# A two-layer graph network on one core: x through two DMA queues, fifteen tiles of rows on VectorE, the destination lists on ScalarE, and chunk 0 summed first

## What is computed

```python
h = jnp.maximum(_layernorm(x, axis=-1), 0.0)
deg = segment_sum(ones, src, N);  dinv = where(deg > 0, rsqrt(max(deg, 1)), 0)
norm = -dinv[src] * dinv[dst]
def cheb_conv(x, W0, W1, b):
    tx1 = segment_sum(x[src] * norm[:, None], dst, N)
    return x @ W0 + tx1 @ W1 + b
h = cheb_conv(h, W1_0, W1_1, b1)
h = layer_norm(h, gamma, beta)
h = where(h >= 0, h, 0.01 * h)
return x + cheb_conv(h, W2_0, W2_1, b2)
```

## Time and profile before

| what | value |
|---|---|
| median of 3 runs | 2083.22 us (2079.54 to 2084.0) |
| profiled execution | 2077.38 us, its span 2075.6 us |
| POOL | 1507.3 us busy, 73% of the span |
| PE | 1742.7 us busy, 84% |
| DVE | 776.0 us busy, 37% |
| ACT | 317.4 us busy, 15% |
| DMA | 514.94 MB, 248 GB/s on average |

### The profile page before, as it was taken

How to read it: one execution, slowest core, us unless ns; L and a number is a source line. 1 busy time by engine, 2 the same in 40 slices (tenths; PEclk the granted TensorE clock), 3 DMA queues, 4 the chain that set the end, 5 groups by cost and what they waited for, 6 DMA issues and landing times.

```text
span 2075.6 us, 25930 instructions
## 1 busy us (share of the span) xinstructions
PE 1742.7 (84%) x8740; PEld 666.3 (32%) x8740; DVE 776.0 (37%) x2411; ACT 317.4 (15%) x647; POOL 1507.3 (73%) x1596
## 2 busy tenths in 40 slices
PE   3459888888888888888888988888898888888888
PEld 3433333332323322223333333333333333323333
DVE  9944444444454444444442222212222222222221
ACT  8701111111111111111111111000110101101010
POOL 2277777777777777777777777777777777777775
PEclk9969999999999999999999999999999999999999
DMA  9898888888888888888878888888888888888875
GB/s 262 267 328 250 244 243 242 243 241 241 236 237 241 243 241 238 237 240 241 243 228 260 256 251 256 251 255 249 253 257 248 253 254 253 256 250 256 255 242 182
DMA packets 188714, 514.94 MB, mean 248 GB/s; under 512 B 45271, under 2 KB 46958, under 8 KB 187339
## 3 DMA queue, kind: packets, MB, share of 16 engines
q0 software_dynamic: 128576, 422.78, 69.2%
q1 hardware_dynamic: 56374, 90.16, 12.5%
q10 hardware_dynamic: 3638, 0.42, 0.3%
HBM read 472.40 MB, written 40.84 MB: 247 GB/s over the span
## 4 chain that ended last, share of the span: by engine, by line
POOL 61%; issue 21%; PE 10%; DVE 6%; DMA 1%; ACT 1%; SPq 0%; DVEq 0%; ACTq 0%
POOL arena L560 61%; PE ps L1232 4%; PE ps L1356 4%; DVE w_all L844 2%; DVE work L844 1%; PE ps L1224 1%; DMA scal<-node_scales 0%; DVE ps L1101 0%; ACT arena L689 0%; DMA arena<-table,idx_all 0%; PE ps L1420 0%; DVE stats L1104 0%; DVE ps L1111 0%; DMA node_scales<-scal_all 0%; DVE stats L853 0%
## 5 line engine op out<-in xcount | busy, mean ns | idle before, releaser
L560 POOL DMA_INDIRECT arena<-table,idx_all x1536 | 1454.8, 947 | 470.5 <-issue 467.4
L1356 PE MATMUL ps<-arena,hots 128*32 128x512 f32 x5048 | 729.1, 611 | 135.6 <-DVE hots L1023 77.2
L1356 PEld LDWEIGHTS ps<-arena,hots 128*32 128x32 f32 x5048 | 186.4, 110 | 653.7 <-issue 458.1
L1023 DVE TENSOR_SCALAR hots<-iota_f,loc_all,arena 128x64 f32<-128x64 f32 (+1 forms) x768 | 234.1, 334 | 341.1 <-DMA arena<-table,idx_all 339.9
L1232 PE MATMUL ps<-arena 128*128 128x512 f32 (+1 forms) x432 | 196.6, 597 | 35.8 <-ACT arena L689 35.8
L1232 PE MATMUL ps<-w_all,arena 128*128 128x512 f32 (+1 forms) x432 | 196.1, 597 | 35.8 <-ACT arena L689 35.8
L679 ACT ACTIVATE arena<-ps,scal 128x512 f32<-128x512 f32 x106 | 73.0, 689 | 921.8 <-PE ps L1420 883.6
L1232 PE MATMUL ps<-arena,work 128*128 128x512 f32 (+1 forms) x432 | 199.5, 605 | 0.0
L1232 PE MATMUL ps<-w_all,work 128*128 128x512 f32 (+1 forms) x432 | 193.2, 591 | 0.0
L1140 DVE SCALAR_TENSOR_TENSOR ps<-ps,scal,arena 128x512 f32<-128x512 f32 x52 | 39.5, 759 | 351.1 <-PE ps L1232 351.1
L1224 PE MATMUL ps<-ident,arena 128*128 128x128 f32 x848 | 137.4, 286 | 27.7 <-DMA scal<-node_scales 20.3
(11 more groups left out here) (158 smaller groups left out, 725.9 us busy)
## 6 DMA issues: line engine op xcount, KB each, us to landing
arena<-table SPq DMA_DIRECT2D x106, 256.0 KB, 4.0
arena<-table,idx_all POOLq DMA_INDIRECT x1550, 4.0
table<-arena SPq DMA_DIRECT2D x53, 256.0 KB, 4.0
arena<-in_x_dram SPq DMA_DIRECT2D x53, 256.0 KB, 5.7
out_dram<-arena SPq DMA_DIRECT2D x53, 256.0 KB
table<-arena SPq DMA_DIRECT2D x10, 1124.4 KB
arena<-in_x_dram POOLq DMA_DIRECT2D x9, 1120.0 KB, 34.0
w_all<-in_L_gnn_W_dram SPq DMA_DIRECT2D x2, 1024.0 KB, 14.0
```

Of the source, the lines that this page charges most:

```text
L560: nc.gpsimd.indirect_dma_start(out=rows_of(n, c)[0:rn, 0:RW if L == 0 else D], out_offset=None, in_=table[L][0:NEAR if near else N, :], in ...
L1023: hot = nc.vector.tensor_scalar(hot_of(n, c)[:, cols], iota_f[:, cols], loc, factor_of(i, c), ALU.is_equal, ALU.mult)
L1356: return nc.tensor.matmul(tx_ps[n % 2][strip, :], hot_of(n, c)[:, strip], rows_of(n, c)[:, 0:D], start=start, stop=stop)
```

## The change

It has seven parts.

1. **x by two queues.** POOL loads only the even groups 2 to 10. SP loads group 0 and all the odd ones, in one go at the start, ahead of the first store to the table. The last group of five is split into three and two tiles, so there are 12 groups.
2. **Fifteen tiles on VectorE**, at the steps 1, 2, and 4 to 16; none after step 16. ScalarE keeps 35.
3. **The dst lists** are converted by ScalarE, between the writing of `idx_all` and its first square root.
4. **The tests of the chunks** in `bases()` take 12 instructions in place of 24: half of them treat three chunks of a group at once.
5. **Loads of SP.** The first weight of layer 0 goes out straight after the factors; the own rows of chunks 0 and 1 come next after the flag, then the second weight, then the wait for the stored scales and the loads of scales.
6. **TensorE** sums chunk 0 before it transposes own rows; it waits for the weights only ahead of the first product.
7. **VectorE** makes all 14 one-hots of chunk 0 before `count_first()`.

```diff
-    XG = (0, 2) + tuple(range(5, NT + 1, 5))
+    XG = (0, 2) + tuple(range(5, NT, 5)) + (NT - 2, NT)
     NG = len(XG) - 1
-    DVE_TILES = (4, 9, 14, 19, 24, 29, 34, 39, 44, 49)
+    DVE_TILES = (4, 9, 14, 18, 19, 23, 24, 28, 29, 33, 34, 39, 43, 44, 49)
-    DVE_AT = (2, 4, 7, 9, 11, 14, 16, 18, 21, 23)
+    DVE_AT = (1, 2, 4, 5, 6, 7, 8, 9, 10, 11, 12, 13, 14, 15, 16)
...
+            for g in range(1, NG, 2):
+                for n0, n1 in parts:
+                    sp.dma_start(nodes[n0:n1, XG[g]:XG[g + 1], :], x_rows[n0:n1, XG[g]:XG[g + 1], :],
+                                 max_dma_last_dim=4 * D).then_inc(s_x[g], 16)
...
+            sp.dma_start(weights[0][0], W10.rearrange("(k p) n -> p k n", p=P)).then_inc(s_w[0], 16)
             sp.wait_ge(s_scales, 1)
             sp.dma_start(node_scales.rearrange("(p t) c -> p (t c)", t=NT),
                          scal_all[:, :, :].rearrange("p t c -> p (t c)")).then_inc(s_scal_out, 16)
-            for k, w in enumerate((W10, W11)):
-                if k:
-
-                    sp.wait_ge(s_group, 1)
-                sp.dma_start(weights[0][k], w.rearrange("(k p) n -> p k n", p=P)).then_inc(s_w[0], 16)
...
+            def load_weights():
+                sp.wait_ge(s_group, 1)
+                sp.dma_start(weights[0][1], W11.rearrange("(k p) n -> p k n", p=P)).then_inc(s_w[0], 16)
+                sp.wait_ge(s_scal_out, 16)
...
             sp.wait_ge(s_base, 1)
-            sp.wait_ge(s_scal_out, 16)
             sp.wait_ge(s_tab, 2 * 16 * (NG - 1))
...
                 if L == 0:
-                    load_own(0, 0)
-                    load_own(0, 1)
+                    load_own(0, 0, False)
+                    load_own(0, 1, False)
+                    load_weights()
+                    load_scales(0, 0, first_node(0))
+                    load_scales(1, 1, first_node(1))
...
-            for g in range(1, NG):
+            for g in range(2, NG, 2):
                 for n0, n1 in ((0, TA), (TA, TR)):
                     pool.dma_start(nodes[n0:n1, XG[g]:XG[g + 1], :], x_rows[n0:n1, XG[g]:XG[g + 1], :],
                                    max_dma_last_dim=4 * D).then_inc(s_x[g], 16)
...
-            pool.wait_ge(s_idxps, 1)
-            pool.wait_ge(s_first, 1)
-            pool.wait_ge(s_dsts, 48)
-            nc.gpsimd.tensor_copy(loc_all[:, 0:FB * P], dst_rows[:, 0:FB * P]).then_inc(s_dstrows, 1)
-            nc.gpsimd.tensor_copy(loc_all[0:S - FB * P, FB * P:],
-                                  dst_rows[0:S - FB * P, FB * P:]).then_inc(s_dstrows, 1)
...
+            act.wait_ge(s_first, 1)
+            act.wait_ge(s_dsts, 48)
+            nc.scalar.copy(loc_all[:, 0:FB * P], dst_rows[:, 0:FB * P]).then_inc(s_dstrows, 1)
+            nc.scalar.copy(loc_all[0:S - FB * P, FB * P:], dst_rows[0:S - FB * P, FB * P:]).then_inc(s_dstrows, 1)
             act.wait_ge(s_vdeg, 1)
...
-                    for j in range(4):
-                        at = c + (SHORT + (j - 1) * SLOTS if j else 0)
-                        setup.add(nc.vector.scalar_tensor_tensor(
-                            out=broken[:, :, j], in0=chunk_begin[:, :, j], scalar=float(strip * Q),
-                            in1=slot_edge[:, :, at], op0=ALU.add, op1=ALU.is_gt if after_it else ALU.is_le))
+                    edge = slot_edge[:, :, SHORT:].rearrange("p g (j c) -> p g j c", c=SLOTS)[:, :, :, c]
+                    test = ALU.is_gt if after_it else ALU.is_le
+                    setup.add(nc.vector.scalar_tensor_tensor(
+                        out=broken[:, :, 0], in0=chunk_begin[:, :, 0], scalar=float(strip * Q),
+                        in1=slot_edge[:, :, c], op0=ALU.add, op1=test))
+                    setup.add(nc.vector.scalar_tensor_tensor(
+                        out=broken[:, :, 1:4], in0=chunk_begin[:, :, 1:4], scalar=float(strip * Q),
+                        in1=edge, op0=ALU.add, op1=test))
...
-                        if i == 0 and c == 5:
+                        if i == 0 and c == SHORT - 1:
                             count_first()
...
                     pe.wait_ge(s_fac, 1)
+                    sums(0, 0)
                 transpose_own(L, 0)
                 transpose_own(L, 1)
+                pe.wait_ge(s_w[L], 32)
                 dense_own(L, 0)
                 for i in range(NC):
-                    if i < NC - 1:
+                    if L == 0 and i == 0:
+                        pass
+                    elif i < NC - 1:
                         sums(L, i)
...
-                pe.wait_ge(s_w[0], 32)
                 layer(0)
-                pe.wait_ge(s_w[1], 32)
                 layer(1)
```

More of the change, by code:

```diff
@@ L386, in _, with load_scales, load_own @@
                          scal_all[:, :, :].rearrange("p t c -> p (t c)")).then_inc(s_scal_out, 16)
-            for k, w in enumerate((W10, W11)):
-                if k:
-                    sp.wait_ge(s_group, 1)
-                sp.dma_start(weights[0][k], w.rearrange("(k p) n -> p k n", p=P)).then_inc(s_w[0], 16)
             def first_node(i):
                 return sp.value_load(base_i[0:1, bass.ds(i, 1)], min_val=0, max_val=BASE_MAX)
-            def load_own(L, i):
+            def load_weights():
+                sp.wait_ge(s_group, 1)
+                sp.dma_start(weights[0][1], W11.rearrange("(k p) n -> p k n", p=P)).then_inc(s_w[0], 16)
+                sp.wait_ge(s_scal_out, 16)
+            def load_scales(u, i, first):
+                sp.dma_start(scal[:, bass.ds(i * NSC, NSC)], node_scales[bass.ds(first, P), :]).then_inc(s_own[u], 16)
+            def load_own(L, i, scales=True):
                 u = (L * NC + i) % 2
@@ L399, in load_own @@
                 sp.dma_start(own[u], table[L][bass.ds(first, P), 0:D]).then_inc(s_own[u], 16)
-                if L == 0:
-                    sp.dma_start(scal[:, bass.ds(i * NSC, NSC)],
-                                 node_scales[bass.ds(first, P), :]).then_inc(s_own[u], 16)
+                if L == 0 and scales:
+                    load_scales(u, i, first)
             def load_residual(i):
@@ L590, in _ @@
                               dst[EC:E].rearrange("(p c) -> p c", c=EC)[:, 0:1]).then_inc(s_nxt, 16)
-            dst_rows = dst.rearrange("(p c) -> p c", p=EP)
+            dst_lists = dst.rearrange("(p c) -> p c", p=EP)
             for n0, n1 in ((0, TA), (TA, EP)):
-                act.dma_start(dst_i[n0:n1, :], dst_rows[n0:n1, :]).then_inc(s_dst, 16)
+                act.dma_start(dst_i[n0:n1, :], dst_lists[n0:n1, :]).then_inc(s_dst, 16)
             act.wait_ge(s_const, 1)
```

1 line of the change is left out of this document (added).

## The result

| | before | after |
|---|---|---|
| median of the runs taken together | 2081.99 us (2079.54 to 2084.0, 4 runs) | 2101.88 us (2098.08 to 2104.01, 4 runs) |
| profiled execution, its span | 2077.38 us, 2075.6 us | 2098.08 us, 2096.3 us |
| start of the gathers of chunk 1 | 117.48 us | 138.53 us |

The ratio is 1.0098 [1.0083, 1.0112], with its 95% interval: the change makes the kernel slower by about 1%. The direction was right and the size was not: the loss is 20 us where 6 were forecast, and lies outside the range.

What follows compares the result with a forecast made beforehand. POOL's gathers were taken to set the pace from chunk 1's start at 117.48 us. Terms +5.6 +2.5 -1.0 delay the flag 7.1 us, and 7.1 - 2.3 + 1.3 gives +6.0: 2089.2 us, range 2083 to 2095.

Steps and rivals of the forecast that it cites:

- x through two queues: VectorE ahead of tile 4: it stalls until group 1 lands from SP's queue, +2.5 us on the flag.
- The bound from above: Tile 4's stall: group 1 lands no later than group 2 did before, 16.20 us, so at most 5.6 us.
- I count no second stall: VectorE's tiles after tile 4: later groups of x arrive in time, no further stall.
- Five tiles, +5.6 us: VectorE's histogram: five more tiles at 1.12 us each delay histogram, factors and flag by 5.6 us.
- The histogram end: VectorE's last histogram operation: forecast 8.1 us later than 96.37, at 104.5 us.
- Twelve tests, -1.0 us: VectorE's chunk tests ahead of the flag: 12 instructions in place of 24 save 1.0 us.
- POOL after the flag: POOL's entry into chunk 1: load of the flag and branch come behind a late flag, 1.26 us.
- Level with the flag, hidden behind it by 0.4 us: Factors in the table before chunk 1: landed by 123.1 us, hidden behind POOL's start at 123.5.
- The gathers of chunk 0: POOL's first gather hangs until the histogram ends at 104.5; all end by 121.9, costing and bringing nothing.
- rival C: Table stores behind SP's loads: starved, the table lands after 105 us; +8.6 us, 2092 us, chance 0.14.
- A (no stall): VectorE ahead of tile 4: x is in time; +3.5 us, 2086.7, no change that can be told, chance 0.27.
- B: Layer 0's first chunks: TensorE sets the pace, so summing chunk 0 early gains some 6 us, about 2077; chance 0.11.

Runs made afterwards that it cites:

- run with ten tiles: Changed kernel with VectorE's ten tiles at the steps of before, x still through two queues: 2087.09 us, ratio 1.0039 to the kernel before.
- gathers last: Changed kernel with x by POOL's queue alone and ten VectorE tiles; POOL also waits for the factors before chunk 0's gathers: 2078.28 us, ratio 0.9998 to before.
- the kernel whose gathers wait: Changed kernel where POOL also waits for the histogram's end before chunk 0's gathers: 2098.66 us, ratio 1.0095 to the kernel before.
- one queue: Changed kernel with x loaded by POOL's queue alone, fifteen VectorE tiles kept: 2088.41 us, ratio 1.0051 to the kernel before.
- the order of before: Changed kernel with chunk 0 summed after the own rows' transposes and first product on TensorE: 2098.45 us, ratio 1.0094 to the kernel before.
- the kernel without parts 1 and 2: Changed kernel with x by POOL's queue alone and VectorE's ten tiles at their old steps: 2078.76 us, ratio 1.0002 to the kernel before.
- the kernel with the flag ahead: Changed kernel with x by POOL's queue, nine VectorE tiles, first weight behind the scales, tests ahead of the factors' one-hots: 2076.63 us, ratio 0.999 to before.

## Why the prediction was wrong in size

**The step that failed is "x through two queues", +2.5 us: it measured 14.1.** Three things were wrong in it.

- *The bound from above was none.* It let tile 4 arrive between "as before" and 16.20, the landing of group 2, "since by then the same lists and groups had been moved". But the order of the groups within the queues is what the change alters: by 16.4 us POOL's queue had moved 1.82 MB, group 2 and part of group 4, in place of SP's group 1. The sum that was wanted is by the queue: 1.68 MB stand in SP's queue up to group 1, and the earlier trace rows gave 222 GB/s for all. An estimate with half of that, 111 GB/s, is 15.1 us and an end past 17, a stall of 6.5 us, above the bound of 5.6. Nothing in the rows spoke for the middle of the two.
- *Share and stragglers.* The queue's bytes were through at 16.4 us, a stall of 5.6: its share was less than half (78 GB/s from 5 to 20 us), but it had a start of 0.84 MB by 5 us. The remaining 4.4 us of the 9.98 passed until the last part of the group had landed. The prediction had no term for this lag, though group 2 had one of 2.4 us before.
- *"I count no second stall."* "Each later group 8 us or so" had no row behind it. The first two groups of SP's queue for which VectorE stood, 1 and 3, came 15.6 us apart (20.78 and 36.38), and VectorE asked for group 3 at step 4: 4.12 us.

**Five tiles, +5.6 us: right.** A step with a tile still lasts 4.17 us. The run with ten tiles finds 13.6 us between the ends of the two histograms, 7.9 of them stalls, and leaves 5.6.

**The histogram end** is the sum: 5.6 + 14.1 = 19.7, less 0.5 for the conversion to `counts` behind step 18, which took 0.74 us beside POOL's own conversion and takes 0.21 now that this one is gone; 19.4 measured. The prediction forecast 8.1 and missed the small gain.

**Twelve tests, -1.0 us: right.** They take 1.40 us where the 24 took from 111.26 to 113.52, 2.26: -0.86.

**The flag, from the end of the histogram:** 19.6 us, where 18.8 - 1.0 = 17.8 was forecast: 1.8 us short. In the run with the gathers last it took 18.0, as forecast. In the change 16 matmuls of the spread of the factors (L1282) last 3.75 us where they last 2.10 before. That term was not in the prediction, and its cause stays open (below).

**"POOL after the flag", 1.26 us: it measured 2.15** (the kernel whose gathers wait) and 2.16 (one queue). The nearest row was VectorE's and not POOL's. Before, the flag was there 2.3 us ahead of chunk 1, so by this step it was ahead by less than 0.2.

**"Level with the flag, hidden behind it by 0.4 us": wrong.** The factors were the last gate, as they were in five of the eleven kernels. The prediction's "landed by about 115" misread its row: the window from 114 to 115 us does not have the last packets of that burst, the next one has 24 more,

```profile
q1 hardware_dynamic: 24, 0.00, 1.4%
```

and the last count came at 116.33, 17.1 us behind the issue and not 15.8. That was one execution, in which the gathers began with the factors; with the gathers ahead they took 18.3 to 21.5. In the change this is worth 138.53 - (135.38 + 2.15) = 1.0 us. From the end of the histogram to chunk 1 it was 117.48 - 96.37 = 21.11 us before and 138.53 - 115.75 = 22.78 after, so of the 21.05 us at the start of chunk 1 19.38 are the end of the histogram and 1.67 all that lies behind it.

**The range.** Its scatter of "2.6 us" and "1.7" below and above is not that of the runs about the median of 2083.2, which is 3.7 and 0.8. With these the range would be 2081.9 to 2094.1; 2101.88 lies outside either.

**The gathers of chunk 0: right.** "I expect the first gather to hang until the histogram ends", + 0.9: it ended 0.96 us behind it, and 0.95 behind it with one queue. The Trainium skill ("SBUF — State Buffer", section "Who interferes with whom") has the rule, an exclusive lock that an instruction with two inputs in SBUF takes from a GpSimd instruction that reads SBUF. The trace agrees: the first gather takes 12.56, 10.38, 7.67, 13.52 and 14.52 us in five kernels, and 1.05 when nothing is in its way, and each time it ends 0.95 to 0.97 us behind the last one-hots. It also shows what the rule leaves open: the gather did not get in between two one-hots either.

**Two queues do not load faster: the rule was right and read too late.** The Trainium skill ("DMA: Bandwidth & Descriptors", section "Issuing engines are not separate DMA queues") gave it, and 246 against 222 GB/s nearly agrees. The prediction used it only for rival C, the stores, and not for its own term, the loads, where it speaks against the middle of the bounds.

**The rivals.** A (no stall) is refuted by 9.98 us. B is refuted by the order of before, 1.0094 against 1.0098. C is half right: the loads do hold up the table (104.15 in place of 99.50, and 108.35 with ten tiles), in part by making ScalarE wait (17.0 us in the change, 3.4 before), which is not the way that C had named. The changed kernel does not pay for it, since the hung gather ends at 116.71 whenever the table lands.

## What to carry to other kernels

When loads are split over queues, add up the bytes that stand ahead of the wanted one in its own queue and divide by that queue's share, which here went by equal numbers of packets and so by their size; the total may hardly grow, so whoever is late gets later. Then add the time until the last part has landed: 2.4 us before, 4.4 and 5.3 with two queues. And when an engine that sets the bound starts behind several gates, list the time of each: here three stood within 2.3 us, and two of them hung on VectorE, so more work for VectorE cost its full length nearly at once, while 10.6 us taken off one gate gave back 0.9.

## What the runs showed of the hardware that was not expected

- Two busy queues on the same 16 DMA engines sent the same number of packets, 460 and 462 in 10 us, and so bytes in the ratio of their packets, 1.55 to 0.91 MB; 333 and 333, and 152 and 152, with SP's packets smaller and then larger than POOL's.
- A group of x was complete 2.4 to 5.3 us after its queue had moved as many bytes, and in the stores of the factors the last two counts of the semaphore came up to 5.4 us behind the others.
- SP's 12 loads of x kept its queue busy with issuing for 44.35 us, from 2.52 to 46.9. All stores of the table stood behind them, the first at 47.00 (before at 21.57).
- The same 16 small fp32 matmuls lasted either 2.0 to 2.1 us (before, and gathers last) or 3.75 us (the other nine). The granted clock does not tell the two apart. The windows of the 4 us from their start, first the change, then the kernel without parts 1 and 2, then with the gathers last; columns as in the earlier trace rows:

```profile
118.76:122.76 4.00, 3.75 (x17) 3.45 (x17) 0.96 (x2) 0.87 (x2) 3.09 (x4) 0.50 1.02 135
```

```profile
99.22:103.22 4.00, 3.75 (x17) 3.46 (x17) 0.96 (x2) 0.87 (x2) 2.94 (x4) 1.00 1.04 123
```

```profile
99.37:103.37 4.00, 2.01 (x17) 1.81 (x17) 2.67 (x5) 0.87 (x2) 2.79 (x3) 0.93 0.62 8
```

The clock is 0.50 in the first, the lower of its two levels (1.2 GHz), and 1.00 in the second (2.4 GHz), and both show 3.75 us. Nor do the gathers tell them apart, for they run in all three, or the traffic (135, 123 and 8 GB/s in the three, but also 8 GB/s in the kernel with the flag ahead, where the matmuls take 3.75 us). What makes the difference was not found; it moves the flag by 1.7 us.
